# The loads of a graph-network kernel's chunk loops are issued from ScalarE's queue in place of SyncE's

## What is computed

```python
def _gat(x, edge_index, W, att_s, att_d, bias, heads, ch, neg_slope):
    h = (x @ W.T).reshape(n, heads, ch)
    a_s = (h * att_s[None]).sum(-1); a_d = (h * att_d[None]).sum(-1)
    logits = jax.nn.leaky_relu(a_s[src] + a_d[dst], neg_slope)
    m = jax.ops.segment_max(logits, dst, num_segments=n)
    ex = jnp.exp(logits - m[dst])
    denom = jax.ops.segment_sum(ex, dst, num_segments=n)
    out = jax.ops.segment_sum((ex / (denom[dst] + 1e-16))[:, :, None] * h[src], dst, num_segments=n)
    return out.reshape(n, heads * ch) + bias
# three of these (heads 2, 2, 1) -> x = layernorm(x + h)
# then per edge: v = relu([x[src], x[dst], edge_attr] @ W1 + b1) @ W2 + b2
# x = layernorm(x + maximum(segment_max(v, dst), x))
```

## Time and profile before

| | |
|---|---|
| median of 3 runs | 19,072.84 us (19,069.2 to 19,077.68) |
| profiled execution | 18,986.31 us |
| its span, first to last instruction | 18,984.6 us |
| POOL busy | 13,804.5 us (73%) |
| DVE busy | 9,849.9 us (52%) |
| PE busy | 5,355.5 us (28%) |
| ACT busy | 2,257.7 us (12%) |

### The profile page before, as it was taken

The page is one execution under the profiler, slowest core; times in us unless marked ns, Lnnn a source line. Parts: engine busy times, 40 slices in busy tenths (PEclk is TensorE's granted clock), DMA queues, the critical chain, the costliest instruction groups (busy, mean ns, idle before and its releaser), DMA issues. The chain is left out here.

```text
span 18984.6 us, 76380 instructions
## 1 busy us (share of the span) xinstructions
PE 5355.5 (28%) x6226; PEld 1523.3 (8%) x6226; DVE 9849.9 (52%) x12316; ACT 2257.7 (12%) x5040; POOL 13804.5 (73%) x13412
## 2 busy tenths in 40 slices
PE   1222222222122222222222222222222333333332
PEld 0000000000000000000000000000000000100000
DVE  3555555555455555555545555555554344444445
ACT  3111111111011111111111111111111000000000
POOL 6777777777677777777677777777766766666665
PEclk9999999999999999999999999999985555555555
DMA  3111111111011111111111111111112222222222
GB/s 92 51 48 51 51 49 51 48 51 47 18 26 26 26 26 26 26 26 26 24 20 26 26 26 26 26 26 26 26 28 61 65 72 67 75 68 69 71 69 53
DMA packets 652143, 812.37 MB, mean 43 GB/s; under 512 B 258009, under 2 KB 427814, under 8 KB 639307
## 3 DMA queue, kind: packets, MB, share of 16 engines
q0 software_dynamic: 433056, 293.09, 9.2%
q1 hardware_dynamic: 106010, 293.26, 4.6%
q10 hardware_dynamic: 113040, 225.69, 3.1%
HBM read 460.64 MB, written 350.42 MB: 43 GB/s over the span
## 5 line engine op out<-in xcount | busy, mean ns | idle before, releaser
L557 POOL DMA_INDIRECT g<-table,idx x9375 | 9954.0, 1062 | 3107.6 <-issue 3107.6
L640 PE MATMUL bank<-ad,ad_sel 4*128 4x512 f32 x2352 | 2212.9, 1088 | 6832.9 <-issue 6761.3
L557 POOL DMA_INDIRECT g<-tablex,idx x3125 | 2992.0, 957 | 1387.0 <-issue 1154.9
L1189 DVE STREAM_TRANSPOSE h_sb<-g 128x512 f32<-128x512 f32 x588 | 607.2, 1033 | 5323.9 <-DMA g<-table,idx 5323.9
L681 PE MATMUL bank<-d_b,w_out 128*128 128x512 f32 (+1 forms) x784 | 709.4, 1058 | 2174.0 <-issue 1877.2
L640 PEld LDWEIGHTS bank<-ad,ad_sel 4*128 4x128 f32 x2352 | 675.6, 316 | 7750.2 <-issue 7674.4
L649 PE MATMUL bank<-h_sb,w_as 128*128 128x512 f32 x1176 | 1216.8, 1138 | 46.2 <-DVE h_sb L1189 46.2
L625 PE MATMUL bank<-r_in,qsel 4*128 4x512 bf16 x784 | 442.9, 565 | 2592.3 <-issue 2434.6
L1285 DVE TENSOR_TENSOR_SCAN s_b<-r_sb,s_b,bank 128x512 f32<-128x512 f32 x196 | 250.0, 1275 | 1526.3 <-remote 1127.3
L700 ACT ACTIVATE r_sb<-bank 128x512 f32<-128x512 f32 x784 | 467.7, 597 | 3959.6 <-issue 2598.2
L675 PE MATMUL bank<-xe_t,w_hid 128*128 128x512 f32 (+1 forms) x784 | 684.3, 980 | 716.4 <-DVE mb L1267 433.9
(11 more groups left out here) (171 smaller groups left out, 6907.3 us busy)
## 6 DMA issues: line engine op xcount, KB each, us to landing
state<-o_sb ACTq DMA_DIRECT2D x585, 288.0 KB
g<-table,idx POOLq DMA_INDIRECT x9375
auxx<-wide SPq DMA_DIRECT2D x97, 1056.0 KB
xd_in<-auxx SPq DMA_DIRECT2D x195, 512.0 KB
xe_t<-in_edge_attr SPq DMA_DIRECT2D x196, 256.0 KB
g<-tablex,idx POOLq DMA_INDIRECT x3125
vmax<-o_sb ACTq DMA_DIRECT2D x195, 256.0 KB
r_in<-rrow SPq DMA_DIRECT2D x784, 4.0 KB
```

The costliest lines, as they stand in the source:

```text
L557: eng.indirect_dma_start(o, None, t[:, :], bass.IndirectOffsetOnAxis(ap=idx[k][:, j:j + 1], axis=0)).then_inc(e_g[k][j // (W // 2)], 16)
L640: last = eng.matmul(p_ad[:, 0:c], ad_sel[:, h, :], view(ad[b], h, [[2, c]], parts=NQ), start=(h == 0), stop=(h == 1))
L1189: v_.transpose(view(h_sb[b], 0, [[1, w], [w, SQ]]), view(g[k], 0, [[F, w], [1, F]])).then_inc(E["tin"], 1)
```

## The change

All loads inside the passes and the fill move from SP's queue to ACT's. SP keeps the loads at the start, the node stages and the output. In an attention pass ACT issues the load of chunk v+3 after the store of chunk v (SP issued it as soon as PE had freed the buffer), and the fill behind it on every second chunk. In the edge network's pass it issues the three loads of chunk v+2 at the end of chunk v. ACT waits for `headw` before the first load of a pass, which SP did. The bytes, the buffers, the semaphores and the instructions of PE, DVE and POOL stay.

```diff
@@ sync
-            for layer in range(3):
-                node(layer)
...
-                def both(i):
-                    steps(i * 2, 0)
-                    steps(i * 2 + 1, 1)
-                    fill_x(i)
...
-            node(3)
...
-            with eng.Fori(1, NI - 1) as i:
-                for k in range(NB):
-                    load_mlp(i * NB + k, k % 2)
...
+            for step in range(5):
+                node(step)
@@ scalar
+            def load_gat(layer, i, k):
+                v, b = i * NB + k, k % 2
+                n = i * NB + (layer * NC + k)
+                need(eng, E["pad"], n - 1)
+                tick(eng, "ticks")
+                eng.dma_start(ad[b][:, 0:cols(v), :].rearrange("q e h -> q (e h)"), quarters(aux, v)).then_inc(E[f"ld{b}"], 16)
+                load_r(v, b, E[f"ld{b}"])
...
+            def load_mlp(v, b):
+                need(eng, M["pre"], v * 2 - 2)
+                tick(eng, "ticks")
+                load_r(v, b, M[f"ld{b}"])
...
                     ends_out(i, k)
+                    if not isinstance(i, int) or i * NB + k + 3 < NC:
+                        load_gat(layer, i if k + 3 < NB else i + 1, (k + 3) % NB)
+                    if layer == 0 and k % 2:
+                        fill_x(i * 2 + k // 2)
+                if layer == 0:
+                    eng.wait_ge(S["rw"], 1 + 16 * 8)
+                eng.wait_ge(D["headw"], 16 * (layer + 1))
+                load_gat(layer, 0, 0)
+                load_gat(layer, 0, 1)
                 restart(0, 0)
                 restart(0, 1)
+                load_gat(layer, 0, 2)
                 refill(0, 0)
...
                     store(v - 1, 1 - b)
+                if not isinstance(v, int) or v + 2 < NC:
+                    load_mlp(v + 2, b)
+
+            eng.wait_ge(D["headw"], 16 * 4)
+            load_mlp(0, 0)
+            load_mlp(1, 1)
             rs(0, 0)
```

More of the change, by code:

```diff
@@ L314, in _ @@
                 eng.dma_start(bass.AP(tensor=rrow.tensor, offset=at, ap=[[NQ * L, HALF], [1, L]]), rbf[:, k, :]).then_inc(S["rw"], 16)
[L316 to L330, removed]
             def node(step):
@@ L371, in node @@
                 eng.wait_ge(D["headw"], 16 * (step + 1))
-            for layer in range(3):
-                node(layer)
[L375 to L390, removed]
-                def both(i):
-                    steps(i * 2, 0)
-                    steps(i * 2 + 1, 1)
-                    fill_x(i)
[L396 to L400, removed]
-            node(3)
[L403 to L415, removed]
-            with eng.Fori(1, NI - 1) as i:
-                for k in range(NB):
-                    load_mlp(i * NB + k, k % 2)
-            for v in range(NC - NB, NC):
-                load_mlp(v, v % 2)
-            node(4)
+            for step in range(5):
+                node(step)
             eng.wait_ge(D["xn"], 5 * NU)
@@ L790, in node, with quarters_r, load_r, fill_x @@
                     skewed(u, u % 2)
+            def quarters_r(v):
+                t = rrow.rearrange("(v q l) w -> v q (l w)", q=NQ, l=L)
+                return t[v, :, :] if isinstance(v, int) else t[bass.ds(v, 1), :, :].rearrange("v q k -> (v q) k")
+            def load_r(v, b, s):
+                eng.dma_start(r_in[b][:, :], quarters_r(v)).then_inc(s, 16)
+            def load_gat(layer, i, k):
[5 more added lines that the diff above has]
+                load_r(v, b, E[f"ld{b}"])
+            wide_v = auxx.rearrange("(p e) c -> p (e c)", p=P)
+            def fill_x(i):
+                w, total = 2112, EL * HID // P
+                assert total // w == NC // 2 - 1
+                eng.dma_start(wide_v[:, i * w:min(total, (i + 1) * w)] if isinstance(i, int) else wide_v[:, bass.ds(i * w, w)],
+                              wide[:, 0:min(w, total - i * w) if isinstance(i, int) else w]).then_inc(S["wide"], 16)
+            def load_mlp(v, b):
+                need(eng, M["pre"], v * 2 - 2)
+                tick(eng, "ticks")
+                load_r(v, b, M[f"ld{b}"])
+                eng.dma_start(chunk_tile(xd_in[b], v, HID), chunk_rows(auxx, v)).then_inc(M[f"ld{b}"], 16)
+                e_ = I["edge_attr_32"]
+                eng.dma_start(xe_t[b][:, :], e_[v, :, :] if isinstance(v, int) else e_[bass.ds(v, 1), :, :].rearrange("v p l -> (v p) l"))\
+                   .then_inc(M[f"ld{b}"], 16)
             for layer in range(3):
@@ L867, in _ @@
                 ends_out(NI - 1, NB - 1)
+                if layer == 0:
+                    fill_x(NC // 2 - 1)
             node(3)
```

## The result

The changed kernel takes 19,315.3 us (median of 4, 19,296.9 to 19,330.8) where the kernel before takes 19,075.3 (median of 4, 19,069.2 to 19,080.5): ratio 1.0126, 95% interval 1.0108 to 1.0143, 240 us slower. Forecast was 17,260 us, and the range ended at 19,100: both the sign and the range are wrong. It went the way of rival (c) in its mild form. Four later sets of runs add a second result that matters more: there the kernel before takes 16,953 to 16,956 us, and in the one that has the changed kernel as it stands the change does nothing, ratio 1.0000 (0.9991 to 1.0009).

A forecast was written before the change was run, and what follows sets the result against it. POOL's gathers were taken as the bound, slowed by a full path shared by SP and DVE. 18,986.3 minus 1,811 us, plus 86.5 for the median of the runs, gave 17,260 us; range 17,130 to 19,100.

The forecast's parts named there:

- rival (c): ACT takes SP's place on the slow path: some +7,000 us, 26,000 us, if all instructions pass there; milder ACT delays 14%.
- POOL's gathers, at two paces: In the passes POOL's gathers set the pace: 1.25 us each at the opening, 1.392 us over pass 1.
- One path that the instructions of SP and DVE pass at 0.70 us each: In mid-pass SP and DVE share a full path; relieving it of SP's instructions was to save 1,811 us.
- 32 x 0.700 = 22.4: In an attention pass, DVE's 23 and SP's 9 instructions a chunk at 0.700 us each give the chunk's period.
- rival (b): Only the last pass or only the attention passes recover: 18,601 or 17,734 us; chance 13%.
- The onset: POOL's first longer gather, 164.5 and 204.4 us into passes 0 and 1, comes when the path's store is full.
- Each pass goes at its opening pace: With the path unsaturated, all four passes keep 1.25 us a gather, 3,905 us a pass, 1,811 us saved.
- ACT's cost: Issuing the loads adds 0.9 or 1.3 us to an attention chunk on ACT, hidden in a gap: zero.
- The slack of the exponentials: ACT's exponentials in attention passes can be late by 9.9 us, 7.5 at a 20.0 us chunk, before DVE waits.
- Loads later: hidden: Attention loads issued almost a chunk later on ACT, landing perhaps 1 or 2 us later, cost nothing.
- (a): Nothing changes: DVE's own work slows POOL and SP is its victim, 19,073 us; 23% together with (d).
- (d): Only the recording is slow at 0.70 us: the profile gets faster, runs stay at 19,073 us; 23% with (a).

The follow-up runs named there:

- e1: Kernel before, with the loads of every pass left out after its first two chunks (fill of pass 0 kept): 18,977.0 us, ratio 0.9997.
- e2: Kernel before, with four more semaphore increments on SP for each chunk: 18,976.7 us, ratio 0.9998.
- set 1: First of five sets of follow-up runs, on one chip, holding e1, e2, e3 and e4; the kernel before takes 18,980.1 us there.
- e4: Kernel before, with eight more semaphore increments on ACT behind its store in each chunk, loads still on SP: 19,179.3 us, ratio 1.0106.
- e9: The changed kernel as it stands, run again beside the kernel before on another set: 16,953.7 us, ratio 1.0000.
- e3: Kernel before, with four more semaphore increments on PE for each chunk: 18,979.3 us, ratio 0.9999.

## Why the prediction was wrong, step by step

*What bounds the kernel: POOL's gathers, at two paces.* Right. 1.25 us a gather is the pace without the steps, and I priced a pass at it with 3,905 us; without the steps it takes 3,900.

*"One path that the instructions of SP and DVE pass at 0.70 us each."* Wrong, and this is the step that failed, with the one I trusted least, that POOL's pace hangs on that path being full. The term it carried was 1,811 us; with SP silent in three of the four passes e1 gains 3 (18,980 to 18,977). It rested on one count, 32 x 0.700 = 22.4, that fitted three passes; the last pass, where it would have asked for 27 us and took 22.4, was already the evidence against it, and I kept it as a remark in rival (b). e1 (23 instructions) and e2 (36) both give 22.4 us. The onset, which I took for the time in which 32 instructions a chunk fill a store, is the same without SP's nine. That DVE and SP are coupled and ACT is not, as I read the rows, falls with it: in the changed kernel ACT has the steps. So the 1,811 us were never there for SP to give; what holds a chunk at 22.4 us in its place no run shows.

*"Each pass goes at its opening pace", and that the runs are no faster than the recorded execution.* The pace after the onset is not a property of this program alone. The same kernel runs at 22.4 us a chunk in set 1 and at 20.0 in the four others; one trace can't show that, and its steps looked like the program's. The 86.5 us that I added for the median were no property of it either: the profiled execution was none of the runs of that median.

*ACT's cost, "I take zero, since ACT's price is measured in the same passes".* Wrong where the steps are on, right where they are not. ACT had 17.5 instructions a chunk in the attention passes before and has 25.1 now (3,328 in 6000 to 9000 us, 132.4 chunks), and with that number it goes in steps of 0.70 us itself. The term I put at nothing measured 240 us, and eight increments alone (e4) 199. A price read at one load was carried to another.

*The slack of the exponentials.* The 9.9 us to L1206 (L1219 before) had the right size, and were for the most part DVE's 9.1 us of waiting for gathers. In the chunk above the exponentials come 10.8 us late; DVE goes on to the next gathered tile at once and then stands still for 9.87 us ahead of L1206 in place of that wait, so the slack is used up and about 1 us passed on. What I had let be late were two issues at 4.2 us each behind the store, 8.4 in all; they take 7.0 (6017.48 to 6024.53). What I had left out lies ahead of the store: its waits and register instructions take steps as well, 8.3 us from L792 (6009.14) to the store's issue. Rival (c) set the point of decision at 0.86 us for each of ACT's 26 instructions, by their sum against 22.4 us. It decides earlier: 25.1 x 0.70 = 17.6 us fits into a chunk, but not into the gap ahead of the exponentials, which stand in the chain from DVE to the index tile and POOL.

*"Loads later: hidden", and the last pass "still hidden" at 12.6 us.* Wrong where the steps are on: DVE waits 1,572 us for `xd_in` and `xe_t` in the last pass, up to 23.9 us at a time. DVE was busy for 1,330 of 3,000 us there before, so most of this falls into time in which it stood still anyway; the pass is 31 us longer. Right without the steps.

*Rivals.* (c), mild, with 14%, is what happened in the result's own runs. (a), 23% together with (d), was right that SP is a victim, and its outcome, no change, is what the sets without the steps give, though for another reason. (b) did not occur. On (d): in both regimes profiled and timed executions agree (18,978 and 18,977 us in e2; 16,952.3 of span and 16,953.7 in e9), but each execution here leaves a span and a clock of its own, so none is surely free of recording. I used that agreement as evidence against recording; it isn't.

*What stays open.* What makes the steps, and why some sets of runs show them and others don't. The sets with and without them are on different chips (that of the result is not known), but no chip was seen at both paces and those with the steps also came first, so chip and time are not told apart; nor is any execution surely free of recording. That the steps come in multiples of 0.70 us, reach POOL only some chunks into a pass, and strike several engines (POOL's gathers and SP before, ACT after, DVE in the last pass) fits a shared outlet behind the engines that fills up. It doesn't say why SP is struck at 9 instructions a chunk and DVE not at 23. The Trainium skill, "NOTIFIC — the notification-queue block", section 7.1 on overflow, says that the internal pipeline of the block that writes trace records holds back its producers rather than lose a record; that would be such an outlet, and no run here shows that it is this one. Against the plain form of it stand e2 and e3, whose additional instructions cost nothing. Also open: whether a gather is limited at 1.40 us or a chunk as a whole at 22.4, and from which number between 17.5 and 25.1 ACT is slowed; the runs for that came out without the steps. No version that does all the gathers beat both kernels: without the steps POOL's 16 x 1.25 us set the time and neither kernel touches them, and with them e1 to e3 are level with the kernel before.

## What to carry to other kernels

A count whose product with a step length gives the period is no cause until a kernel with another count has been tried; when one stage of the same trace contradicts it, drop it there. If register instructions that take 0.04 us have a median of 0.70 us, look at a trace of the same program from another chip and another time before you tune for it: here the engine under the steps gained nothing from relief, and 2,026 us (18,980 - 16,954), 11 per cent, lay in the steps. And before work is moved to an engine in the chain between the others, measure its slack at the place where the work goes in: eight trivial instructions on ACT cost 199 us with the steps on, and the change's own loads cost nothing with them off.

## What the runs showed that I had not expected

- One program, two paces: 18,980 to 19,075 us on two sets of runs, 16,953 to 16,956 on four others, each steady within 0.2%. The passes take 4,350 or 3,900 us.
- With the steps on, an engine can change its price with the number of its instructions: ACT's register instruction went from 43 ns to 699 (the change, 25.1 instructions a chunk) and 700 (e4, 25.5) from 17.5. DVE, with 23, kept medians of 21 to 63 ns for its queue instructions in pass 1 of the kernel before.
- Eight semaphore increments behind each of 12,500 gathers (some 100,000 more instructions on POOL) took no time that can be measured, with the steps off.
